# State space chunks: ScalarE scales both batches' states ahead of its copy of batch 0's transposes

## The chip, the cores and the metric

One core of a Trainium2 chip runs the whole program in one launch. The metric is the device time of one execution in microseconds (us). Three executions of the kernel before took 903.69, 904.62 and 905.2 us; the median is 904.62 us.

## The reference

The program is a stack of four blocks over x (2 batches, 1024 positions, 256 features) and a context of 2 x 77 x 256: a gated recurrence with attention and a feed-forward net, an attention block with a bottleneck of four features, an attention with 16 heads, and a last block whose first half is the state space layer (Mamba-2) that this change touches:

```
def step(h, inp):
    dec, u, bt, ct = inp
    h = h * dec[:, :, None, None] + u[..., None] * bt[:, None, None, :]
    y = jnp.einsum('bhpn,bn->bhp', h, ct)
    return (h, y)
...
y = ys.transpose(1, 0, 2, 3) + D_skip[None, None, :, None] * xh
u = _rms(y.reshape(b, L, D_INNER) * jax.nn.silu(z), gnorm_w)
return resid + u @ out_proj_w
```

There are 8 heads of 64 channels with a state of 64 x 128 each, so one batch's state is 128 x 512 numbers. dec is exp(dt * A), one factor for each head and position.

## The kernel before

Activations lie feature-major: features on the 128 partitions, positions along the free dimension. The positions are worked through in two halves (j = 0, 1) of T = 512, and the state space layer cuts each half into four chunks of 128 positions (s = 0 to 3). Within a chunk the recurrence is done with matrices: a masked 128 x 128 decay matrix for each head gives what the chunk's own positions contribute, and the state carried over from the chunk before gives the rest. Both batches (b = 0, 1) go through together, each with its own four PSUM banks and its own tiles.

The order of the work is written out by hand in a generator, mamba_order, which every engine's program walks through: for each s the pieces s1 (b = 0), s1 (b = 1), s2 (0), s2 (1), s3 (0), s3 (1). Each engine takes its share of each piece in that order and waits on semaphores for the others. What each engine does in a piece for one batch:

- s1, TensorE: four transposes of the convolved input (L1477), one transpose of B and the product of B and C (L1479, L1480), then four short bf16 matmuls that build the exponents of the decay matrix. It waits for this batch's L2481 of the chunk before (semaphore yr).
- s1, ScalarE: in the kernel before, first the decay: eight instructions of 128x64 (L1931) write SE = STATE times one factor for each head; they wait for the new state (L2476, semaphore s7). Then XT = the copy of the transposes out of PSUM (L1937), BT = the copy of B's transpose (L1939), and the exponential of the decay matrix, 128x1024 (L1941).
- s1, GpSimd: WX = XT times a factor (L822, 128x512); it waits for the copy L1937 and is waited for by TensorE's state update in s2. XT, WX and the factors WM all lie in SBUF.
- s2, VectorE: the decay matrix times the product of B and C (L2470), the carried part of y (L2472), and STATE = SE + the new contribution in PSUM (L2476; L2478 in the very first chunk). TensorE: four matmuls with the state (they wait for L1941 and for L2476 of the chunk before), then one with BT and WX.
- s3, TensorE: eight matmuls with the decay matrices (after L2470). VectorE: L2481 adds them to y out of PSUM, four scalar_tensor_tensor instructions of 128x128 (L2485) add D_skip times x, and L2487 multiplies by the gate. L2485 and L2487 each read two tensors from SBUF; L2470, L2472, L2476 and L2481 read one from SBUF and one from PSUM. A self-wait stands between L2472 and L2476, between L2481 and L2485, and between L2485 and L2487.

In the first chunk of the second half (j = 1, s = 0) both batches' decays already come together, after batch 1's exponential; they serve that same chunk. The first chunk of all (j = 0, s = 0) has no decay. So six chunks have the decay at the head of s1: s = 1, 2, 3 of either half.

After the four chunks of a half, piece "out" squares, normalises and projects the result.

Of the kernel before, what the change touches and what calls it, by code (L numbers as in the profile page):

```python
# [112 lines left out]
def xattn_stack_kernel(nc, xT, ctxT, mask, maskc, vecs, m0, m1, m2, rows6, consts, outT):  # L113
    vcol, nvec, mats, sizes = layout()
    with ExitStack() as ctx:
# [65 lines left out]
        def sem(name):  # L181
            name = home.get(name, name)
            if name not in sems:
                sems[name] = ctx.enter_context(nc.semaphore(name))
            return sems[name]

        def after(name, n):

            return sem(name), n + before.get(name, 0)
# [20 lines left out]
        def cn(name, rows=P):  # L210
            return CN[0:rows, CONST[name][0]:CONST[name][1]]
# [230 lines left out]
        def bank(b, k):  # L442
            return ps[:, 4 * b + k, :]
# [4 lines left out]
        def part_of(q):  # L448

            return q % B, slice(q // B * T, (q // B + 1) * T)  # L450
# [5 lines left out]
        BS = range(B)  # L456
# [278 lines left out]
        def inbank(b, j, k):  # L735

            return bank(b, (k + 2) % 4 if (j, b) == (0, 0) else k % 4)

        def of(name, b):

            return name + "01"[b]
# [821 lines left out]
        def _(act):  # L1563
# [194 lines left out]
            for q in UNITS[B:]:  # L1758
                b, span = part_of(q)
# [23 lines left out]
            for q in UNITS[:B]:  # L1783
                b, span = part_of(q)
                act.wait_ge(*after("rep_mm", q + 1))
                nc.scalar.activation(USR[:, b, span], ps[:, q, :], ACT.Copy).then_inc(sem("us"), 1)
            for q in UNITS[B:]:
                b, span = part_of(q)
# [60 lines left out]
            for piece, b, j, s in mamba_order():  # L1849
# [16 lines left out]
                elif piece == "xm":  # L1866
                    for u in BS:
                        act.wait_ge(*after("norm_xc", CENTRED["x3"] + B + u + 1))
                        nc.scalar.activation(ST[u], XC[u], ACT.Square).then_inc(sem("norm_sq"), 1)
                elif piece == "xq":  # L1870
                    for u in BS:
                        act.wait_ge(*after("norm_ms", NORMS["x3"] + B + u + 1))
                        nc.scalar.activation(RTB[u], bank(1, u), ACT.Ln, bias=cn("eps5")).then_inc(sem("norm_ln"), 1)
                        act.wait_ge(*after("norm_ln", NORMS["x3"] + B + u + 1))
                        nc.scalar.activation(RTB[u], RTB[u], ACT.Exp, scale=-0.5).then_inc(sem("norm_rt"), 1)
                elif piece == "sq":
                    act.wait_ge(*after("x3", 4 * J))
                    for u in BS:
                        nc.scalar.activation(SQ7[u], X[:, :, u, T:2 * T], ACT.Square).then_inc(sem("norm_sq"), 1)
                elif piece == "nb":  # L1880
                    for u in BS:
                        act.wait_ge(*after("norm_ms", NORMS["r3"] + u + 1))
                        nc.scalar.activation(RT7[u], ps[:, 6 + u, :], ACT.Ln, bias=cn("eps5")).then_inc(sem("norm_ln"), 1)
                        act.wait_ge(*after("norm_ln", NORMS["r3"] + u + 1))
                        nc.scalar.activation(RT7[u], RT7[u], ACT.Exp, scale=-0.5).then_inc(sem("norm_rt"), 1)
                elif piece == "dt":
                    act.wait_ge(sem("dt1"), 1)
                    nc.scalar.activation(ETR, ETR, ACT.Exp, scale=-1.0).then_inc(sem("et"), 1)
                    act.wait_ge(sem("et"), 1)
                    nc.scalar.activation(ETR, ETR, ACT.Ln, bias=cn("ones")[:, 0:1]).then_inc(sem("l1p"), 1)  # L1890
                elif piece == "rows":
                    prep_act(act, "a3")
                    act.wait_ge(sem("rows_mm"), 1)
                    nc.scalar.activation(RN[0], ps[:, 6, :], ACT.Copy).then_inc(sem("ltm"), 1)
                    act.wait_ge(sem("rows_mm"), 2)
                    nc.scalar.activation(WM.rearrange("p s n -> p (s n)"), ps[:, 5, :], ACT.Copy)
                    act.wait_ge(sem("een_mm"), 1)
                    nc.scalar.activation(EEN.rearrange("p s n -> p (s n)"), ps[:, 7, :], ACT.Exp).then_inc(sem("een"), 1)
                elif piece == "sel":
                    act.wait_ge(*after("sel_mm", j + 1))  # L1900
                    for i in range(4):
                        nc.scalar.activation(BX[j][:, i, :], ps[:, 3, :], ACT.Identity, bias=cn("unit")[:, i:i + 1], scale=cn("pick")[:, i:i + 1])
                    nc.scalar.activation(AE[j], ps[:, 3, :], ACT.Identity, bias=cn("first"), scale=cn("later")).then_inc(sem("ab"), 1)
                elif piece == "gate":
                    def convolved(b):
                        act.wait_ge(*after(of("cv", b), XBC * (j + 1)))
                        nc.scalar.activation(CV[b][:, 0:4, :], CV[b][:, 0:4, :], ACT.Silu)  # L1907
                        nc.scalar.activation(CV[b][:, 4:XBC, :], CV[b][:, 4:XBC, :], ACT.Silu).then_inc(sem(of("xs", b)), 1)

                    if j == 0 and b:  # L1910
                        convolved(0)
                    for c in range(4):
                        act.wait_ge(*after(of("in_mm", b), 10 * j + XBC + c + 1))
                        nc.scalar.activation(ZF[b][:, c, :], inbank(b, j, XBC + c), ACT.Silu).then_inc(sem(of("iev", b)), 1)
                        if b and c == (1 if j else 0):
                            convolved(1)
                    if j and b == 0:
                        convolved(0)
                    if b or j == 0:
                        nc.scalar.preload_act_table_set("natural_log_exp_and_others")  # L1920
                elif piece == "ef":
                    act.wait_ge(*after(of("ef_mm", b), j + 1))
                    for k in (2, 0):
                        nc.scalar.activation(EF[b][:, k:k + 2, :], ps[:, 4 * b + k:4 * b + k + 2, :], ACT.Exp).then_inc(sem(of("ef", b)), 1)  # L1924
                elif piece == "s1":
                    def decay(b):
                        act.wait_ge(*after(of("s7", b), n))
                        for h in range(HM):
                            head = slice(h * PD, (h + 1) * PD)
                            col = 32 * (B * j + b) + h  # L1930
                            ins = nc.scalar.activation(SE[b][:, head], STATE[b][:, head], ACT.Copy, scale=EEN[:, s, col:col + 1])  # L1931
                        ins.then_inc(sem(of("se", b)), 1)

                    if s:
                        decay(b)
                    act.wait_ge(*after(of("xt_mm", b), n + 1))
                    nc.scalar.activation(XT[b], bank(b, 0), ACT.Copy).then_inc(sem(of("dtx", b)), 1)  # L1937
                    act.wait_ge(*after(of("g7_mm", b), n + 1))
                    nc.scalar.activation(BT[b], bank(b, 1)[:, 0:P], ACT.Copy).then_inc(sem(of("bt", b)), 1)  # L1939
                    act.wait_ge(*after(of("dm_mm", b), n + 1))  # L1940
                    nc.scalar.activation(DM[b], ps[:, 4 * b + 2:4 * b + 4, :].rearrange("p k (h n) -> p (k h) n", h=4), ACT.Exp).then_inc(sem(of("dme", b)), 1)  # L1941
                    if s == 0 and j and b:
                        for u in BS:
                            decay(u)
                elif piece == "out":
                    act.wait_ge(*after(of("y7", b), SUB * j + SUB))
                    nc.scalar.activation(EF[b], ZF[b], ACT.Square).then_inc(sem(of("sq", b)), 1)
                    if j and b == 0:
                        act.wait_ge(sem("l3_ms"), B)
                        for u in BS:  # L1950
                            nc.scalar.activation(RTL[u], RTL[u], ACT.Ln, bias=cn("eps5")).then_inc(sem("l3_ln"), 1)
                        act.wait_ge(sem("l3_ln"), B)
                        for u in BS:
                            nc.scalar.activation(RTL[u], RTL[u], ACT.Exp, scale=-0.5).then_inc(sem("norm_rt"), 1)
                    act.wait_ge(*after(of("ms", b), j + 1))
                    nc.scalar.activation(RN[b], bank(b, 0), ACT.Ln, scale=1.0 / DI, bias=cn("eps5")).then_inc(sem(of("rl", b)), 1)
                    act.wait_ge(*after(of("rl", b), j + 1))
                    nc.scalar.activation(RN[b], RN[b], ACT.Exp, scale=-0.5).then_inc(sem(of("rr", b)), 1)
# [647 lines left out]
```

## Time and profile before

| what | value |
|---|---|
| median of three runs | 904.62 us |
| profiled execution, its own time | 905.31 us |
| its span | 903.2 us |
| mean granted TensorE clock | 0.994 of full speed |
| TensorE matmul busy | 840.6 us (93%) |
| VectorE busy | 517.3 us (57%) |
| ScalarE busy | 450.2 us (50%) |
| GpSimd busy | 48.5 us (5%) |
| L1931, the decay: 112 instructions | 28.0 us, mean 342 ns |
| L822, WX: 16 instructions | 1040 to 1380 ns, median 1042 ns |

Span is the time from the first to the last instruction; the execution's own time includes what lies around it. Busy shares are averages over the whole program, most of which is not the state space layer; the chunks take about 40 us in either half (from 655 to 696 us and from 757 to 801 us of the span). A row of the timeline gives the start, the duration, the engine and line, what is written from what, how many instructions were merged, and in brackets the idle time before it and what ended that. PEld is TensorE's loading of weights.

### The profile page before, as it was taken

What the parts mean: (1) busy time and instruction counts of PE and PEld (TensorE: products, weight loads), DVE (VectorE), ACT (ScalarE), POOL (GpSimd) and SP (SyncE); (2) the same over time, 40 slices, a digit from 0 to 9 for tenths busy, and PEclk for the clock granted to TensorE, in tenths of its full rate; (3) what the DMA queues carried; (4) which work ended last, traced back from release to release, by engine and by line L of the source; (5) the groups of instructions that cost most, each with busy time, mean ns of one, the idle gap of its engine ahead of it and who ended that gap; (6) DMA issues with size and microseconds to landing.
All of it is one profiled execution on the core that took longest, in us unless ns stands there. A gap on an engine that the chain in (4) does not pass through costs nothing.

```text
span 903.2 us, 10354 instructions
## 1 busy us (share of the span) xinstructions
PE 840.6 (93%) x4287; PEld 384.5 (43%) x4290; DVE 517.3 (57%) x714; ACT 450.2 (50%) x662; POOL 48.5 (5%) x41
## 2 busy tenths in 40 slices
PE   6998999999899999998898998999888999888987
PEld 2545444444344445453324244234455444544342
DVE  3378999843431031177636035479789495984442
ACT  3785222554434125353442723657875568652634
POOL 1000000020000000012200000000021000210000
PEclk9998999999999999999999999999999999999999
DMA  7000000011000000030000000000000000000011
GB/s 293 1 1 1 0 0 1 20 75 46 2 0 1 0 1 0 1 139 0 1 1 2 1 1 1 1 0 1 0 2 1 0 1 1 1 1 1 1 48 47
DMA packets 3005, 15.62 MB, mean 17 GB/s; under 512 B 656, under 2 KB 912, under 8 KB 2320
## 3 DMA queue, kind: packets, MB, share of 16 engines
q1 hardware_dynamic: 2816, 12.88, 3.8%
q0 software_dynamic: 144, 2.10, 0.6%
q8 instruction: 34, 0.56, 0.3%
q14 instruction: 11, 0.09, 0.0%
HBM read 12.87 MB, written 2.10 MB: 17 GB/s over the span
## 4 chain that ended last, share of the span: by engine, by line
PE 71%; ACT 15%; DVE 10%; DMA 2%; issue 1%; SPq 0%; POOL 0%; DVEq 0%; ACTq 0%
PE ps L421 70%; DVE VB L669 3%; ACT AR L653 3%; DMA WA<-in_m 2%; ACT AR L1941 2%; ACT AR L1931 1%; DVE AR L2254 1%; ACT AR L1625 1%; DVE AR L685 1%; ACT AR L1907 1%; ACT AR L658 1%; ACT AR L656 1%; DVE AR L511 1%; ACT AR L1924 1%; ACT AR L1937 1%
## 5 line engine op out<-in xcount | busy, mean ns | idle before, releaser
L421 PE MATMUL ps<-AR,WA 128*128 128x512 f32 (+2 forms) x716 | 307.8, 594 | 6.2 <-DVE AR L2487 3.6
L421 PEld LDWEIGHTS ps<-AR,WA 128*128 128x128 f32 (+2 forms) x716 | 130.4, 188 | 172.1 <-issue 157.6
L421 PE MATMUL ps<-AR,CN 128*128 128x512 f32 (+3 forms) x304 | 102.5, 598 | 2.8 <-DVE AR L1990 1.2
L421 PE MATMUL ps<-AR 128*64 128x128 f32 (+4 forms) x704 | 96.8, 402 | 6.2 <-ACT AR L1941 2.0
L685 DVE TENSOR_TENSOR AR<-ps,AR 128x512 f32<-128x512 f32 x24 | 16.6, 692 | 99.4 <-ACT AR L658 99.4
L421 PEld LDWEIGHTS ps<-AR 128*64 128x64 f32 (+3 forms) x704 | 51.1, 158 | 44.0 <-issue 19.4
L653 ACT ACTIVATE AR<-ps 77x2048 f32<-77x2048 f32 x24 | 44.0, 1870 | 42.2 <-PE ps L421 31.1
L669 DVE TENSOR_REDUCE VB<-ps 128x16 f32<-128x1232 f32 x32 | 44.9, 1438 | 29.4 <-PE ps L421 28.6
L421 PEld LDWEIGHTS ps<-AR,CN 128*128 128x128 f32 (+2 forms) x304 | 35.3, 157 | 50.9 <-issue 35.1
L2384 DVE SCALAR_TENSOR_TENSOR AR<-AR,VC 128x512 f32<-128x512 f32 x72 | 50.6, 749 | 5.4 <-ACT AR L1865 4.4
L1642 ACT ACTIVATE AR<-ps 128x512 f32<-128x512 f32 (+1 forms) x40 | 23.8, 597 | 59.1 <-DVE AR L2099 36.1
L421 PE MATMUL ps<-KB,WA 128*128 128x512 f32 (+1 forms) x120 | 51.4, 594 | 0.9 <-ACT AR L1924 0.9
L1739 ACT ACTIVATE AR<-ps,VC 128x512 f32<-128x512 f32 x32 | 21.9, 687 | 56.0 <-PE ps L421 56.0
L421 PE MATMUL ps<-CN 128*128 128x204 f32 (+6 forms) x102 | 41.0, 510 | 8.9 <-DMA CN<-in_consts 5.2
L2172 DVE SCALAR_TENSOR_TENSOR X<-ps,VC,X 128x512 f32<-128x512 f32 x8 | 5.6, 747 | 58.5 <-PE ps L421 58.5
L421 PE MATMUL ps<-AR,VS 77*32 77x512 f32 x256 | 32.4, 601 | 4.0 <-ACT AR L653 3.9
L421 PEld LDWEIGHTS ps<-KB,WA 128*128 128x128 f32 (+1 forms) x120 | 21.5, 184 | 29.4 <-issue 27.8
L421 PE MATMUL ps<-VB,CN 32*77 32x512 f32 x256 | 33.2, 587 | 0.0
L1931 ACT ACTIVATE AR<-AR,VB 128x64 f32<-128x64 f32 x112 | 28.0, 342 | 4.3 <-DVE AR L2476 2.9
L2099 DVE TENSOR_TENSOR_SCAN AR<-AR 128x512 f32<-128x512 f32 x24 | 29.5, 1272 | 0.4
L421 PEld LDWEIGHTS ps<-CN 128*128 128x128 f32 x102 | 17.9, 200 | 25.9 <-issue 13.0
L2470 DVE TENSOR_TENSOR AR<-AR,ps 128x1024 f32<-128x1024 f32 x16 | 19.4, 1216 | 15.9 <-ACT AR L1941 15.9
(334 smaller groups left out, 1126.0 us busy)
## 6 DMA issues: line engine op xcount, KB each, us to landing
WA<-in_m SPq DMA_DIRECT2D x1, 2856.0 KB, 9.7
WA<-in_m SPq DMA_DIRECT2D x1, 2560.0 KB, 15.6
X<-in_xT POOLq DMA_DIRECT2D x1, 2048.0 KB, 9.3
WA<-in_m SPq DMA_DIRECT2D x1, 2048.0 KB, 8.8
out<-X SPq DMA_DIRECT2D x4, 512.0 KB, 3.1
WB<-in_m SPq DMA_DIRECT2D x1, 1024.0 KB, 4.8
AR<-in_rows SPq DMA_DIRECT2D x1, 640.0 KB, 9.9
WA<-in_m SPq DMA_DIRECT2D x1, 512.0 KB, 16.4
```

The source lines that it names most:

```text
L421: return nc.tensor.matmul(out, lhsT, rhs, start=first, stop=last)
L511: nc.vector.tensor_tensor(xc[b], src(b), bc(at(b, 0), DC, 1), ALU.subtract).then_inc(sem("norm_xc"), 1)
L653: nc.scalar.activation(PTX[b][:, k], ps[0:M, 4 * b:4 * b + 4, :], ACT.Exp, bias=bias).then_inc(sem("att_ex"), 1)
L669: nc.vector.tensor_reduce(where[:, :, :, i] if PARTS[p] == 1 else where[:, :, 2 * k:2 * k + 2, 2 * g:2 * g + 2], ps[:, 4 * b:4 * b + 4, 0: ...
L685: nc.vector.tensor_tensor(ST[b][:, g, :], bank(b, 0), RTB[b], ALU.mult).then_inc(sem("att_ctx"), 1)
L1642: nc.scalar.activation(to[b][mo], bank(b, 2 * jj + mo), ACT.Sigmoid).then_inc(sem("g"), 1)
L1739: nc.scalar.activation(FH[b][item], bank(b, i % 2), ACT.Gelu_apprx_tanh, bias=v("bf1", item)).then_inc(sem("ff"), 1)
L1931: ins = nc.scalar.activation(SE[b][:, head], STATE[b][:, head], ACT.Copy, scale=EEN[:, s, col:col + 1])
L1941: nc.scalar.activation(DM[b], ps[:, 4 * b + 2:4 * b + 4, :].rearrange("p k (h n) -> p (k h) n", h=4), ACT.Exp).then_inc(sem(of("dme", b)), 1)
L2099: nc.vector.tensor_tensor_scan(dst[:, mo, b, jj, span], aa[b][:, mo, :], gz[b][:, mo, :], first, ALU.mult, ALU.add).then_inc(sem("h"), 1)
L2384: ins = STT(out=CV[b][:, k, :], in0=XB[b][:, k, tap:tap + T], scalar=v("convw", 4 * k + tap), in1=CV[b][:, k, :], op0=ALU.mult, op1=ALU.add)
L2470: TT(DM[b], DM[b], bc(bank(b, 1)[:, P:2 * P], HM, 1), ALU.mult).then_inc(sem(of("dm", b)), 1)
```

## The change

In the chunks s = 1, 2, 3 of either half, ScalarE issues both batches' decays ahead of batch 0's copy of the transposes, and none ahead of batch 1's. In s1 of batch 0 it therefore now also waits for batch 1's L2476 of the chunk before. Nothing else is changed; the first chunks of the halves stay as they are.

```
                     if s:
-                        decay(b)
...
+                    for u in BS if s and b == 0 else ():
+                        decay(u)
                     act.wait_ge(*after(of("xt_mm", b), n + 1))
                     nc.scalar.activation(XT[b], bank(b, 0), ACT.Copy).then_inc(sem(of("dtx", b)), 1)
```

(The line `if s:` is removed along with the call under it.) The function decay(b), unchanged:

```
def decay(b):
    act.wait_ge(*after(of("s7", b), n))
    for h in range(HM):
        head = slice(h * PD, (h + 1) * PD)
        col = 32 * (B * j + b) + h
        ins = nc.scalar.activation(SE[b][:, head], STATE[b][:, head], ACT.Copy, scale=EEN[:, s, col:col + 1])
    ins.then_inc(sem(of("se", b)), 1)
```

## Rows read from the trace of the kernel before

**Rows 1.** The chain that ended last, from 770 to 800 us, shares by line

```profile
by line: PE ps L421 40.6%; ACT AR L1941 19.4%; ACT AR L1931 19.0%; ACT AR L1937 4.8%; PE ps L1477 3.9%; DVE AR L2485 3.8%; DVE AR L2487 2.3%; DVE AR L2476 2.3%; DVE AR L2481 2.3%; ACT AR L1939 1.6%; DVE AR L2472 1.1%; issue 0.9%; PE ps L147
```

**Rows 2.** Timeline of one chunk: start, us, engine, line, count, [idle before <-releaser]

```profile
777.04 0.69 DVE L2476 TENSOR_TENSOR AR<-AR,ps 128x512 f32<-128x512 f32 x1
777.71 0.69 DVE L2481 TENSOR_TENSOR AR<-AR,ps 128x512 f32<-128x512 f32 x1
778.43 1.14 DVE L2485 SCALAR_TENSOR_TENSOR AR<-AR,VC 128x128 f32<-128x128 f32 x4
...
778.47 0.66 PE L1477 MATMUL ps<-CN,AR 128*128 128x128 f32 x4
...
779.16 0.60 ACT L1937 ACTIVATE AR<-ps 128x512 f32<-128x512 f32 x1 [1.83 <-PE ps L1477]
779.61 0.69 DVE L2487 TENSOR_TENSOR AR<-AR 128x512 f32<-128x512 f32 x1
...
779.83 1.36 POOL L822 TENSOR_TENSOR AR<-AR,VB 128x512 f32<-128x512 f32 x1 [5.22 <-ACT AR L1937]
780.22 0.68 DVE L2481 TENSOR_TENSOR AR<-AR,ps 128x512 f32<-128x512 f32 x1
780.25 1.02 ACT L1941 ACTIVATE AR<-ps 128x1024 f32<-128x1024 f32 x1 [0.32 <-PE ps L421]
780.93 1.20 DVE L2485 SCALAR_TENSOR_TENSOR AR<-AR,VC 128x128 f32<-128x128 f32 x4
...
780.95 0.66 PE L1477 MATMUL ps<-CN,AR 128*128 128x128 f32 x4 [0.75 <-DVE AR L2481]
781.17 2.01 ACT L1931 ACTIVATE AR<-AR,VB 128x64 f32<-128x64 f32 x8
```

**Rows 3.** The same chunk's timeline, its second half

```profile
782.17 0.69 DVE L2487 TENSOR_TENSOR AR<-AR 128x512 f32<-128x512 f32 x1
...
782.78 1.21 DVE L2470 TENSOR_TENSOR AR<-AR,ps 128x1024 f32<-128x1024 f32 x1
783.08 0.58 ACT L1937 ACTIVATE AR<-ps 128x512 f32<-128x512 f32 x1
...
783.74 1.04 POOL L822 TENSOR_TENSOR AR<-AR,VB 128x512 f32<-128x512 f32 x1 [2.54 <-ACT AR L1937]
783.91 0.69 DVE L2472 TENSOR_TENSOR AR<-ps,AR 128x512 f32<-128x512 f32 x1
784.73 0.69 DVE L2476 TENSOR_TENSOR AR<-AR,ps 128x512 f32<-128x512 f32 x1
784.78 1.19 PEld L421 LDWEIGHTS ps<-AR 128*128 128x128 f32 x10 [0.97 <-ACT AR L1941]
785.34 1.21 DVE L2470 TENSOR_TENSOR AR<-AR,ps 128x1024 f32<-128x1024 f32 x1
785.46 2.02 ACT L1931 ACTIVATE AR<-AR,VB 128x64 f32<-128x64 f32 x8 [0.73 <-DVE AR L2476]
786.47 0.68 DVE L2472 TENSOR_TENSOR AR<-ps,AR 128x512 f32<-128x512 f32 x1
...
787.19 0.69 DVE L2476 TENSOR_TENSOR AR<-AR,ps 128x512 f32<-128x512 f32 x1
```

**Rows 4.** Timeline elsewhere: a long GpSimd instruction and a VectorE instruction behind it

```profile
415.54 5.04 POOL L810 TENSOR_TENSOR X<-X,AR 128x2048 f32<-128x2048 f32 x1 [12.96 <-ACT AR L1778]
```

**Rows 5.** VectorE's timeline at that instruction's end

```profile
419.77 0.96 DVE L2249 TENSOR_SCALAR WA<-WA,VC 128x256 f32<-128x256 f32 x1
```

**Rows 6.** All of line L2249: duration ns min/median/max, first and last start

```profile
L2249 DVE TENSOR_SCALAR WA<-WA,VC x4: 341/342/962, 419.8 to 421.2; 128x256 f32<-128x256 f32 x4
```

**Rows 7.** Timeline of the second half's start, chunks s = 0 and 1

```profile
762.34 5.85 ACT L1931 ACTIVATE AR<-AR,VB 128x64 f32<-128x64 f32 x24
...
770.07 0.68 DVE L2481 TENSOR_TENSOR AR<-AR,ps 128x512 f32<-128x512 f32 x1
...
770.78 1.20 DVE L2485 SCALAR_TENSOR_TENSOR AR<-AR,VC 128x128 f32<-128x128 f32 x4
```

More of the change, by code:

```diff
@@ L1932, in decay @@
                         ins.then_inc(sem(of("se", b)), 1)
-                    if s:
-                        decay(b)
+                    for u in BS if s and b == 0 else ():
+                        decay(u)
                     act.wait_ge(*after(of("xt_mm", b), n + 1))
```

## The prediction

> **What bounds the kernel now.** I read three views. The chain of waits through the second half's chunks [rows 1] puts 19.0% on the decay (L1931) and 19.4% on the exponential behind it (L1941). That is the case for the change: TensorE's weight load for batch 1's state matmuls sits idle 0.97 us until L1941 of batch 1 is done, at 784.78 [rows 3], that exponential and its copy follow the decay of batch 1 (781.17 to 783.18) [rows 2, 3], and ScalarE itself idles 1.83 us ahead of batch 0's copy at 779.16 [rows 2]. Moving 2 us of decay into that hole looks like a gain of 0.97 us in each of six chunks, 5.8 us.
>
> The second view, VectorE's timeline over one chunk [rows 2, 3], says otherwise. Its twelve groups start 0.67, 0.72, 1.18, 0.61, 0.71, 1.24, 0.61, 1.13, 0.82, 0.61, 1.13 and 0.72 us after each other, from L2476 of batch 1 (777.04) round to the next (787.19): 10.15 us, with no hole. An unhindered step behind a 0.69 us instruction is 0.61 us (779.61 to 780.22) or, where a self-wait stands between, 0.72 us (786.47 to 787.19). So only two places wait for somebody: L2481 of batch 0 (0.67 for 0.61, on TensorE) and L2476 of batch 0 (0.82 for 0.72, on TensorE's state update). VectorE is the bound; the chain view followed a cycle that is within 0.2 us of VectorE's, and shows only the one that came last.
>
> The third view is GpSimd's two instructions in the same rows. WX of batch 1 (783.74) takes 1.04 us; WX of batch 0 (779.83) takes 1.36 us, beside L2487 of batch 0 (779.61 to 780.30). It ends at 781.19, which is 1.04 us after 780.15: it stood still until 0.15 us before L2487's record ended. L2487 lost nothing (0.69 us, as the other one at 782.17). Then the first of batch 1's four L2485 starts while WX still runs (780.93 against 781.19), and the four take 1.20 us where batch 0's take 1.14: 0.06 us lost.
>
> **The change step by step.** Take the same chunk and keep L2476 of batch 1 at 777.04.
>
> 1. Removed: the decay between batch 0's exponential and batch 1's copy. Batch 1's copy can start when its transposes are done, and the exponential when its exponents are: TensorE's weight load no longer waits 0.97 us. What is late next is VectorE, which isn't moved by that except at L2481 of batch 0: up to 0.06 us gained. The 0.10 us at L2476 of batch 0 stays, since its state update follows batch 1's transposes in TensorE's queue, and those follow L2481 of batch 1. Without anything else the chunk would take 10.09 us, and six chunks give 0.36, about 0.4 us.
>
> 2. Added: batch 1's decay ahead of batch 0's copy. It waits for L2476 of batch 1, which ends at 777.73, plus 0.04 us (784.73 + 0.69 to 785.46): start 777.77. Batch 0's decay is over by then (785.46 + 1.91 is before 787.19 + 0.69). From the decay's start to the copy's is 1.91 us (781.17 to 783.08), so batch 0's copy starts at 779.68 instead of 779.16, 0.52 us late. Queued behind it on ScalarE are B's copy and the exponential of batch 0, now ending about 781.4; TensorE wants that exponential only after batch 1's exponents, some 1.3 us after the 780.95 start of its transposes, so this is hidden. Who waits for the copy itself is GpSimd.
>
> 3. Moved with it: WX of batch 0. It starts 0.66 us after the copy (783.08 to 783.74): 780.34. L2487 of batch 0 now stands at 779.55 to 780.24, so WX is no longer held up, and ends at 781.38 instead of 781.19. Batch 1's L2485 starts at 780.87. What does it lose? Two rows bound it. Before, an overlap of 0.26 us cost 0.06, which as a share (0.23) makes 0.12 us of the new overlap of 0.51. At the other end is a GpSimd instruction at 415.54 that ends at 420.58 [rows 4], with a VectorE instruction behind it that starts at 419.77 and takes 0.96 us [rows 5] where the same line otherwise takes 0.34 [rows 6]: it stood still 0.62 us, until 420.39, which is 0.19 us before GpSimd's record ends. By that reading, L2485 stands still until 781.38 - 0.19 = 781.19, 0.32 us. It fits the small loss too: 781.19 - 0.19 is 781.00, and L2485 should have begun at 780.93, which is 0.07. I take 0.32.
>
> 4. Moved as well: WX of batch 1. Batch 1's L2481 stands at 780.16, its transposes start 0.73 later (780.22 to 780.95), the copy 0.69 after that (778.47 to 779.16), WX 0.67 after that: 782.25. L2487 of batch 1 comes at 780.87 + 0.32 + 1.17 = 782.36. GpSimd is ahead by 0.11 us. L2487, with both inputs in SBUF, then stands still until 782.25 + 1.04 - 0.19 = 783.10: 0.74 us. Before, this WX ran at 783.74 beside L2470 and L2472, which have one input in PSUM and lost nothing (1.21 and 0.69 us with it and without it). The bounds are nothing, if L2487 gets in first, and 0.85, if GpSimd is a whole release ahead; 0.74 is the one that the timing gives.
>
> So VectorE's round becomes 10.15 - 0.06 - 0.10 (both waits are swallowed) - 0.07 + 0.32 + 0.74 = 10.98 us, 0.83 more. Everything in it is counted from L2476 of batch 1, so it repeats; five of the six chunks have this pattern: 4.15 us.
>
> 5. The sixth, s = 1 of the second half. There ScalarE is behind: 24 decays in a row end at 768.19 [rows 7]. Eight more end past 770.0, batch 0's copy starts at 770.00 and WX at 770.66, while L2485 comes at 770.78: it stands still until 771.51, 0.73 us. Batch 1's WX then starts at about 772.23, amid the four L2485, and stops the next one until 773.08, some 0.77 us. That is 1.50 - 0.07 - 0.16 = 1.27 us.
>
> **Sum**: 4.15 + 1.27 = 5.4 us. Nothing hides it: TensorE's output projection waits for the last L2487, and TensorE is busy nearly without a break from there on. Against the profiled execution, 905.31 becomes 910.7; that execution lies 0.7 above the median, so the forecast is 904.62 + 5.4 = 910.0 us. TensorE's clock stands at 0.994 on average with waits of this length in the chunks already; I price it at nothing.
>
> The step that the rows leave open is the small overlap in 3: it can be read as a share or as a lock. The Trainium skill, SBUF — State Buffer, section "Who interferes with whom", says that a VectorE instruction with two SBUF inputs contends with a GpSimd instruction that reads SBUF, that the first to issue holds the shared ports for its whole length, and that the other blocks. By that rule the sum is the 5.4 us above; by a share it is rival B. The trace agrees with the rule in the 0.62 us stop [rows 5, 6], though there with a tensor_scalar.
>
> **Rivals.**
>
> A. L2487 of batch 1 gets in ahead of WX. The margin is 0.11 us, built from five steps read to 0.01 us each, and GpSimd's spans are rough. Then only 0.32 is lost: 10.24 us a chunk, 0.09 more, times five, plus the 1.27 of step 5: +1.7 us, 906.3. For it: the small margin. Against: L2485's own stop pushes L2487 back by the 0.32 that decides the race; below 0.21 it would turn.
>
> B. VectorE and GpSimd share rather than lock. Losing 0.23 of each overlap, L2485 gives 0.12 and L2487 0.16: 9.92 + 0.28 = 10.20, +0.05 a chunk, or at the other end nothing lost and the 0.36 of step 1 gained. Time 904.2 to 905.2. Against it: L2487 lost nothing while WX lost 0.32, and the 0.62 us stop.
>
> C. The chain view is right, and the 0.97 us comes off each chunk: 898.8 us. Against it: VectorE's round has 10.15 us with only 0.16 of waits and 0.07 of stop. Even with all of them gone it is 9.92, which caps the gain at 6 x 0.23 = 1.4 us, 903.2. It would need VectorE's steps to shrink.
>
> That the change doesn't do what it says would need batch 1's state to be late; it ends 1.4 us before the copy was due, so the decays do move.
>
> **How the numbers follow.** A measurement of this kernel can tell about 0.2%, 1.8 us, from no change. Forecast 0.64, A 0.13, B 0.19, C 0.04. Slower by over 0.2%: the forecast and a quarter of A, 0.67. Same: the rest of A and B, 0.29. Faster: C, 0.04. The range reaches from B's middle, 904.5, through A to 911.4, the forecast with 0.85 in place of 0.74 in five chunks (0.55) and the spread of the runs (0.75). The forecast's own range is 908.3 to 911.4.
>
> **What would show it.** Right: the first L2485 of batch 1 at about 0.67 us for 0.35 and L2487 of batch 1 at about 1.4 us for 0.69; both WX at 1.04 us; about 11.0 us from chunk to chunk; TensorE's wait on batch 1's L1941 gone, and a longer one on L2481. Wrong: L2487 of batch 1 at 0.69 us with a WX of over 1.3 us beside it (A), or a round of 10.1 us (B), or of 9.9 or less (C).

## The result and the profile after

The changed kernel takes 913.42 us in the median of seven executions (910.48 to 915.59), against 905.17 us for the kernel before on the same chips. The ratio is 1.0083, with a 95% interval from 1.0059 to 1.0107: 8.2 us slower, where 5.4 were forecast and the range ended at 911.4. The direction and the mechanism in the chunks hold; the size does not, since a term that was put at nothing is missing.

| what | before | after |
|---|---|---|
| profiled execution, its own time | 905.31 us | 915.59 us |
| its span | 903.2 us | 913.4 us |
| mean granted TensorE clock | 0.994 | 0.987 |
| VectorE busy | 517.3 us | 522.6 us |
| ScalarE busy | 450.2 us | 450.7 us |

The timeline of one chunk after, in the second half, from the L2476 of batch 1 that starts the count to the next one [answers to rows 2 and 3]:

```profile
782.43 0.69 DVE L2476 TENSOR_TENSOR AR<-AR,ps 128x512 f32<-128x512 f32 x1
783.04 0.68 DVE L2481 TENSOR_TENSOR AR<-AR,ps 128x512 f32<-128x512 f32 x1
783.15 2.02 ACT L1931 ACTIVATE AR<-AR,VB 128x64 f32<-128x64 f32 x8 [0.43 <-DVE AR L2476]
783.75 1.14 DVE L2485 SCALAR_TENSOR_TENSOR AR<-AR,VC 128x128 f32<-128x128 f32 x4
...
784.93 0.69 DVE L2487 TENSOR_TENSOR AR<-AR 128x512 f32<-128x512 f32 x1
785.08 0.57 ACT L1937 ACTIVATE AR<-ps 128x512 f32<-128x512 f32 x1
...
785.54 0.68 DVE L2481 TENSOR_TENSOR AR<-AR,ps 128x512 f32<-128x512 f32 x1
...
785.73 1.04 POOL L822 TENSOR_TENSOR AR<-AR,VB 128x512 f32<-128x512 f32 x1 [8.39 <-ACT AR L1937]
786.25 1.46 DVE L2485 SCALAR_TENSOR_TENSOR AR<-AR,VC 128x128 f32<-128x128 f32 x4
...
787.64 1.04 POOL L822 TENSOR_TENSOR AR<-AR,VB 128x512 f32<-128x512 f32 x1 [0.87 <-ACT AR L1937]
787.74 1.49 DVE L2487 TENSOR_TENSOR AR<-AR 128x512 f32<-128x512 f32 x1
...
791.00 0.69 DVE L2476 TENSOR_TENSOR AR<-AR,ps 128x512 f32<-128x512 f32 x1
...
793.45 0.69 DVE L2476 TENSOR_TENSOR AR<-AR,ps 128x512 f32<-128x512 f32 x1
```

Read it against [rows 2, 3]. WX of batch 0 (785.73) now takes 1.04 us instead of 1.36 and ends at 786.77. Batch 1's four L2485 take 1.46 us instead of 1.20: 0.32 more than batch 0's undisturbed 1.14. WX of batch 1 starts at 787.64, L2487 of batch 1 0.10 us behind it at 787.74, and that takes 1.49 us for 0.69. From one L2476 of batch 1 to the next are 11.02 us, 10.15 before. GpSimd gained, VectorE lost: both WX have their shortest time, and every VectorE instruction with two SBUF inputs that begins beside one waits until it is nearly done. By the 0.19 us of the working L2487 would end at 789.18 (787.64 + 1.04 - 0.19 + 0.69); its record ends at 789.23, so it went on only 0.14 us before WX's record ends.

The chunk s = 1 of the second half, where ScalarE is behind [rows 7]:

```profile
766.41 7.76 ACT L1931 ACTIVATE AR<-AR,VB 128x64 f32<-128x64 f32 x32
...
774.72 1.04 POOL L822 TENSOR_TENSOR AR<-AR,VB 128x512 f32<-128x512 f32 x1 [8.11 <-ACT AR L1937]
774.86 2.63 DVE L2485 SCALAR_TENSOR_TENSOR AR<-AR,VC 128x128 f32<-128x128 f32 x4
...
776.27 1.06 POOL L822 TENSOR_TENSOR AR<-AR,VB 128x512 f32<-128x512 f32 x1 [0.51 <-ACT AR L1937]
```

The four L2485 take 2.63 us, 1.49 more than undisturbed (1.50 in the working), stopped once by each WX.

So far everything is as forecast. One chunk of this trace is not: in s = 1 of the first half GpSimd lost the race.

```profile
668.14 0.69 DVE L2487 TENSOR_TENSOR AR<-AR 128x512 f32<-128x512 f32 x1
...
668.29 1.44 POOL L822 TENSOR_TENSOR AR<-AR,VB 128x512 f32<-128x512 f32 x1 [1.12 <-ACT AR L1937]
```

WX of batch 1 came 0.15 us behind L2487, and it is WX that was stopped (1.44 us); the four L2485 took 1.21 us, and the chunk 10.09 us instead of 11.02. TensorE's clock was low just ahead of it (0.50 from 655 to 660 us), VectorE waited for TensorE, and so came to its instructions at other moments against GpSimd's. So in this execution the chunks cost 4.7 us more than before, not 5.4.

The rest is outside the chunks. TensorE's timeline behind the last chunk of each half, first before, then after:

```profile
695.85 3.70 PE L421 MATMUL ps<-AR,WA 128*128 128x512 f32 x8 [1.82 <-DVE AR L2487]
...
800.67 3.70 PE L421 MATMUL ps<-AR,WA 128*128 128x512 f32 x8 [1.81 <-DVE AR L2487]
```

```profile
698.44 5.40 PE L421 MATMUL ps<-AR,WA 128*128 128x512 f32 x8 [2.73 <-DVE AR L2487]
...
807.72 5.40 PE L421 MATMUL ps<-AR,WA 128*128 128x512 f32 x8 [2.73 <-DVE AR L2487]
```

The same eight matmuls of the output projection take 5.40 us instead of 3.70, in both halves. TensorE waited 2.73 us ahead of them instead of 1.8: its work in the last chunk is done earlier, since it no longer waits for batch 1's exponential, while VectorE's L2487 of batch 0 comes when VectorE gets there. Busy time by stretch, with the granted clock in the column behind the engines, for the changed kernel:

```profile
695.00:700.00 5.00, 2.27 (x17) 1.30 (x14) 4.86 (x13) 1.58 (x1) 0.00 (x0) 0.94 0.00 0
700.00:705.00 5.00, 5.00 (x10) 2.00 (x9) 1.99 (x3) 0.33 (x1) 0.00 (x0) 0.72 0.00 0
805.00:810.00 5.00, 2.28 (x4) 1.16 (x5) 4.86 (x13) 2.31 (x2) 0.00 (x0) 0.86 0.00 0
810.00:815.00 5.00, 5.00 (x10) 2.01 (x9) 3.66 (x4) 2.11 (x5) 1.80 (x1) 0.80 0.02 3
```

In the kernel before the stretches around these matmuls stand at 1.00. Here the clock went from 2.4 to 1.2 GHz behind TensorE's wait (cut into single microseconds: 1.00 up to 699, 0.50 from 700 to 702) and came back during the projection (1.00 from 703). This trace also has such a stretch from 655 to 660 us (0.50), ahead of anything that the change moves; the kernel before has some of its own, in other places (0.73 to 0.92 between 70 and 85 us). They come and go from execution to execution, and single times of one kernel scatter over 6 us and more with them (an execution of the kernel before at a clock of 0.997 took 902.3 us, one at 0.984 took 911.5). The profiled executions differ by 10.3 us, the medians by 8.2.

### The profile page after: what moved, and what is told of

The parts are those of the page before. It is cut to its first block, busy times and chain, and to the rows that moved or that the text cites. A ratio compares the mean times of both kernels' runs of the same rounds, so it can differ in the third digit from the quotient of the medians.

```text
span 913.4 us, 10357 instructions
## 1 busy us (share of the span) xinstructions
PE 846.1 (93%) x4290; PEld 387.5 (42%) x4290; DVE 522.6 (57%) x714; ACT 450.7 (49%) x662; POOL 47.1 (5%) x41
## 4 chain that ended last, share of the span: by engine, by line
PE 71%; DVE 15%; ACT 11%; issue 2%; DMA 1%; SPq 0%; POOL 0%; DVEq 0%; ACTq 0%
PE ps L421 69%; DVE VB L669 3%; ACT AR L653 3%; DMA CX<-in_ctxT 1%; DVE AR L2485 1%; DVE AR L2254 1%; DVE AR L2481 1%; DVE AR L2470 1%; ACT AR L1625 1%; DVE AR L2476 1%; DVE VB L2099 1%; DVE AR L685 1%; DVE AR L2487 1%; ACT AR L1907 1%; ACT AR L658 1%
## 5 line engine op out<-in xcount | busy, mean ns | idle before, releaser
L421 PE MATMUL ps<-AR,WA 128*128 128x512 f32 (+2 forms) x716 | 311.2, 599 | 6.9 <-DVE AR L2487 5.5
L421 PE MATMUL ps<-AR,CN 128*128 128x512 f32 (+3 forms) x304 | 104.4, 604 | 2.9 <-DVE AR L1990 1.2
L421 PE MATMUL ps<-AR 128*64 128x128 f32 (+4 forms) x704 | 99.1, 407 | 6.4 <-ACT AR L1941 2.0
L421 PEld LDWEIGHTS ps<-AR 128*64 128x64 f32 (+3 forms) x704 | 53.6, 162 | 44.0 <-issue 21.9
L2470 DVE TENSOR_TENSOR AR<-AR,ps 128x1024 f32<-128x1024 f32 x16 | 19.4, 1214 | 15.9 <-ACT AR L1941 15.9
```

The costliest lines, as they stand in the source:

```text
L421: return nc.tensor.matmul(out, lhsT, rhs, start=first, stop=last)
L2470: TT(DM[b], DM[b], bc(bank(b, 1)[:, P:2 * P], HM, 1), ALU.mult).then_inc(sem(of("dm", b)), 1)
```

## The experiments

Each run was timed beside the kernel before on the same chip; ratios have 95% intervals. "A chunk" is the time from one L2481 of batch 0 to the next, in steady state: 10.16 us before, 11.02 in the changed kernel. Unless something else is said the edit is made to the changed kernel.

### Does GpSimd's WX stop VectorE?

**e1_gate_wx1** makes WX of batch 1 wait for L2487:

```
+                    if b and 4 * j + s:
+                        pool.wait_ge(*after(of("y7", 1), 4 * j + s))
                     nc.gpsimd.tensor_tensor(h3(WX[b]), ...
```

> The changed kernel, with one wait more: GpSimd's WX of batch 1 waits for VectorE's L2487 of batch 1 of the chunk before. Lock theory (an instruction of GpSimd and one of VectorE with two SBUF inputs exclude each other, first come first served): L2487 of batch 1 back from 1.49 to 0.69 us, the four L2485 of batch 1 still at 1.46, chunk to chunk 10.24 us instead of 11.02, no stop of 0.8 in the chunk s = 1 of the second half. In the chunks 4.4 us less than the changed kernel. If the cost of the clock behind the chunks hangs on TensorE's wait of 2.7 us there, which this edit leaves as it is, it stays: about 4 us above the kernel before; if that was chance, about 1 us above. Rival (the order of ScalarE's work itself costs the time, by way of TensorE): nothing gained over the changed kernel, 8 us above before.

Measured: 907.24 us, ratio 1.0025 (1.0009 to 1.004), about 1.8 us above before. A chunk takes 10.22 us; the chunk s = 1 of the second half takes 10.6. In its timeline, where the lines stand two further down (L2487 is the four additions, L2489 the gate product):

```profile
770.41 1.04 POOL L824 TENSOR_TENSOR AR<-AR,VB 128x512 f32<-128x512 f32 x1 [8.11 <-ACT AR L1939]
770.55 1.83 DVE L2487 SCALAR_TENSOR_TENSOR AR<-AR,VC 128x128 f32<-128x128 f32 x4
...
772.42 0.69 DVE L2489 TENSOR_TENSOR AR<-AR 128x512 f32<-128x512 f32 x1
...
773.25 1.04 POOL L824 TENSOR_TENSOR AR<-AR,VB 128x512 f32<-128x512 f32 x1 [1.80 <-DVE AR L2489]
```

The gate product is back at 0.69 us in all sixteen places; the stop of the four additions by WX of batch 0 stays (1.83 here, 1.46 in the other chunks but the first half's s = 1, which again stands behind a stretch at the lower clock, with 1.20). One added wait gives back 0.80 of the 0.86 us a chunk. ScalarE's order is unchanged in this run, so the order by itself isn't what costs the time. The wait behind the chunks came out at 2.28 and 2.29 us, not at the 2.7 that the text assumed, and the eight matmuls behind both took 3.70 us; the total lies between the text's two cases.

**e2_gate_both** makes both WX wait (the same two lines without `b and`).

> The changed kernel, with both WX waiting for L2487 of batch 1 of the chunk before. Lock theory: no VectorE instruction is held up any more: L2485 of batch 1 at 1.14 and L2487 at 0.69 us; but WX of batch 0 is now late for TensorE's state update, L2476 of batch 0 waits some 0.4 us, and a chunk takes about 10.4 us. 1.7 us above the kernel before, plus 3 if the clock falls behind the chunks. Rival: as the changed kernel.

Measured: 909.65 us, ratio 1.0047 (1.0023 to 1.0071). No VectorE instruction is held up: 1.14 and 0.69 us everywhere. But a chunk takes 10.60 us, since L2476 of batch 0 now waits for WX by way of TensorE:

```profile
785.15 2.04 POOL L824 TENSOR_TENSOR AR<-AR,VB 128x512 f32<-128x512 f32 x2 [8.56 <-DVE AR L2489]
786.05 0.68 DVE L2474 TENSOR_TENSOR AR<-ps,AR 128x512 f32<-128x512 f32 x1
786.25 4.78 PE L421 MATMUL ps<-AR 128*128 128x512 f32 x44 [0.26 <-POOL AR L824]
787.47 0.69 DVE L2478 TENSOR_TENSOR AR<-AR,ps 128x512 f32<-128x512 f32 x1 [0.73 <-DVE AR L2474]
```

The 0.73 us ahead of 787.47 is that wait (the view names the instruction in front of it). The forecast of 10.4 was 0.2 low. Behind the chunks TensorE waited 2.14 us twice, and once the eight matmuls took 5.40 us.

**e3_wx_memset** takes the reading away from GpSimd:

```
-                    nc.gpsimd.tensor_tensor(h3(WX[b]), h3(XT[b]), bc(WM[...], PD, 2), ALU.mult)...
+                    nc.gpsimd.memset(WX[b], 0.0)...
```

> The changed kernel with WX written by a memset of the same shape instead of the product (leaves out the product of XT and its factors, so the state stays zero): GpSimd reads nothing from SBUF. Lock theory: L2485 of batch 1 at 1.14 and L2487 at 0.69 us wherever the memset runs, a chunk takes 10.09 us, 0.4 us below the kernel before over the six chunks; plus 3 us if the clock falls behind the chunks, since TensorE's wait there stays near 2.7 us. Rival (a delay from ScalarE's order): a chunk still takes 11.0 us.

Measured: 905.33 us, ratio 1.0009 (0.9984 to 1.0034). A chunk takes 10.08 us (10.09 expected):

```profile
766.99 0.53 POOL L822 MEMSET AR<- 128x512 f32 x1 [8.63 <-ACT AR L1937]
767.14 1.14 DVE L2485 SCALAR_TENSOR_TENSOR AR<-AR,VC 128x128 f32<-128x128 f32 x4
...
776.68 0.52 POOL L822 MEMSET AR<- 128x512 f32 x1 [7.62 <-ACT AR L1937]
...
777.22 1.14 DVE L2485 SCALAR_TENSOR_TENSOR AR<-AR,VC 128x128 f32<-128x128 f32 x4
...
778.39 0.69 DVE L2487 TENSOR_TENSOR AR<-AR 128x512 f32<-128x512 f32 x1
...
778.59 0.53 POOL L822 MEMSET AR<- 128x512 f32 x1 [1.39 <-ACT AR L1937]
```

The pair at 766.99, in the chunk s = 1 of the second half, is the test: the memset was there first, the additions began 0.15 us behind it, and they take 1.14 us, where a stop until 0.20 us before the memset's end would have cost 0.18. In the chunk at 776.68 the first memset ends just ahead of the additions, so there the shorter instruction does as much as the missing read. The second begins 0.20 us behind L2487, which would have won against a WX as well; it shows that a memset isn't stopped in its turn (0.53 us). With GpSimd out of the way the new order is worth 0.08 us a chunk: that is all that TensorE's 0.97 us of waiting had ever cost.

**e7_split** cuts batch 1's decay in two, so that neither WX moves into VectorE's way (the edit is shown against the kernel before; the helper takes the heads as a second argument):

```
+                    if s and b == 0:
+                        decay(0)
+                        decay(1, range(4))
+                    elif s:
+                        decay(1, range(4, HM))
```

> The changed kernel with batch 1's decay cut in two: four heads ahead of batch 0's copy, four ahead of batch 1's. Batch 0's copy is then no later than in the kernel before, and batch 1's copy comes 0.5 us later than in the changed kernel, so that its WX would start about 0.05 us behind L2487 of batch 1. Lock theory: L2487 of batch 1 at 0.69 us, WX of both batches at 1.36 us, the four L2485 of batch 1 at 1.20, a chunk takes 10.09 us: 0.4 us below the kernel before. If WX of batch 1 gets in first after all, L2487 shows 1.4 us and a chunk 10.9. Rival (ScalarE's order costs the time): a chunk between 10.2 and 11.0 with no long VectorE instruction.

Measured: 907.21 us, ratio 1.0026 (0.9997 to 1.0056). Inside the chunks it is as expected to 0.02 us: 10.07 to 10.08 us a chunk, the additions of batch 1 at 1.21, the gate product at 0.69. Here WX of batch 0 came behind the gate product of batch 0 and waited for it:

```profile
789.34 0.69 DVE L2491 TENSOR_TENSOR AR<-AR 128x512 f32<-128x512 f32 x1
...
789.56 1.38 POOL L822 TENSOR_TENSOR AR<-AR,VB 128x512 f32<-128x512 f32 x1 [6.08 <-ACT AR L1941]
```

WX of batch 1 started only as the gate product of batch 1 ended, and took 1.04 us, where 1.36 was expected. The total isn't what the chunks give: it lies 2.2 us above the kernel before, where 0.4 below was expected. The mean granted clock of its twelve runs was 0.990, and the 0.5 us that the chunks gained can't be seen beside that.

### Where do the other 2 us come from?

**a1_after_again** is the changed kernel once more; **a2_after_look** and **a3_after_look** are one traced execution of it each.

> The changed kernel once more, for a second trace and for its clock beside that of the kernel before on one chip. Lock theory: 11.02 us from chunk to chunk, 11.4 into the chunk s = 1 of the second half, L2487 of batch 1 at 1.49 us in five chunks or, if the half's start is delayed by the clock, in four. Clock theory: a mean granted clock some 0.002 to 0.003 below the kernel before, and of the two waits of 2.7 us behind the chunks at least one followed by eight matmuls that take 5.4 us instead of 3.7; about 8 us above the kernel before. Rival (the clock's share of the first measurement was chance): the same clock as before, and 5.5 us above.

> The changed kernel, one look for the clock behind the chunks. Clock theory: of the two waits of 2.7 us for L2487 at least one is followed by a fall of the granted clock, eight matmuls in 5.4 us instead of 3.7.

> As a2_after_look: a fall behind at least one of the two waits of 2.7 us. If three or more of the four waits of these two looks show none, the clock falls there by chance, and the cause of its share stays open.

Measured: 912.52 us, ratio 1.008 (1.0054 to 1.0106); the two single executions took 913.53 and 912.38 us. The trace of a1_after_again has no stretch at the lower clock ahead of or in its chunks, and so shows their price cleanly: 11.01, 11.01, 11.02 us in the first half and 11.39, 11.01, 11.02 in the second, for 10.13, 10.16, 10.16 and 10.14, 10.16, 10.16 before. That is 5.55 us more; the forecast had 5.42. Behind its chunks:

```profile
695.14 3.70 PE L421 MATMUL ps<-AR,WA 128*128 128x512 f32 x8 [2.72 <-DVE AR L2487]
...
802.91 5.40 PE L421 MATMUL ps<-AR,WA 128*128 128x512 f32 x8 [2.73 <-DVE AR L2487]
```

Over the four traces of the changed kernel there are seven waits of 2.72 to 2.73 us, and five are followed by matmuls at the lower clock (an eighth was 2.11 us long, since TensorE's clock had fallen in the chunk ahead of it). Two waits a run, five times in seven, 1.7 us each, is 2.4 us. Over all its 19 runs the mean granted clock is 0.9903, that of 95 runs of the kernel before, beside the experiments, 0.9932; the medians are 912.66 and 905.05. The difference of 7.6 us less 5.5 leaves 2.1, or 2.5 if the first half's s = 1 escapes the stops in half of the executions, as in two of the four traces (10.09 and 10.08 us). a3_after_look shows one more place where the clock falls: in the last chunk of its second half the four transposes of batch 1 took 1.12 us instead of 0.66, L2487 came ahead of WX (0.69 us, with a WX of 1.24 us beside it), and the chunk took 13.25 us instead of 11.02, as VectorE waited for TensorE. In e4_spare_again, below, the same chunk took 11.66 us. Two of the seven traces with chunks of 11.0 us have such a fall behind a half's first chunk; neither of the two traces with the order of the kernel before has (before, e6_before_spare). That the fall comes for certain, which the first text expected of at least one wait a run, is refuted by a3_after_look: none there behind its one wait of 2.7 us.

**e4_spare**, **e4_spare_again** and **e8_one_spare** give TensorE something to do in that wait, matmuls of 512 columns whose result nobody reads (e8 has one `spare(3, T)` instead of the loop of two):

```
                     last.then_inc(sem(of("y1_mm", b)), 1)
+                    if s == SUB - 1 and b:
+                        pe.wait_ge(*after(of("s7", 0), n + 1))
+                        for u in range(2):
+                            spare(3, T)
```

> The changed kernel with two spare matmuls of 512 columns on TensorE at the end of each half's last chunk, into a bank nobody reads. Clock theory (the granted clock falls behind the chunks since TensorE waits 2.73 us for L2487, 1.8 before): TensorE's wait there is about 1.0 us, the first eight matmuls of the output projection take 3.7 us (5.4 in the changed kernel), the clock of those stretches is 1.00, and the kernel is some 3 us faster than the changed one: 5.4 us above the kernel before. The chunks stay at 11.02 us. Rival (the clock falls at random): no steady gain over the changed kernel.

> The changed kernel with two spare matmuls at the end of each half's last chunk, measured again for its clock. If TensorE's wait of 2.7 us there is what lowers the clock (19 runs of the changed kernel have a mean of 0.9903, 82 of the kernel before 0.9932): a mean clock of 0.992 to 0.993 and 6 us above the kernel before. If the longer waits inside the chunks lower it: 0.990 to 0.991 and 8 us above.

> The same with one spare matmul instead of two, so that TensorE's wait is 1.7 to 1.8 us, as in the kernel before. If that wait decides: the eight matmuls behind it take 3.7 us, a mean clock of 0.992 to 0.993, and 6 us above the kernel before. If not: as the changed kernel, 8 us above.

Measured: 910.59 us, ratio 1.006 (1.0038 to 1.0081); 910.91 us, ratio 1.006 (1.0038 to 1.0081); 910.57 us, ratio 1.0057 (1.0038 to 1.0077). With two spares the wait is 0.81 us (once 0.23, behind a chunk under a lower clock), and the projection's eight matmuls take 3.70 us in all four places traced. Those of e4_spare:

```profile
698.35 3.70 PE L421 MATMUL ps<-AR,WA 128*128 128x512 f32 x8 [0.81 <-DVE AR L2491]
...
806.13 3.70 PE L421 MATMUL ps<-AR,WA 128*128 128x512 f32 x8 [0.81 <-DVE AR L2491]
```

The chunks stay at 11.0 us. The 21 runs of the three have a mean clock of 0.9929 and a median of 910.6 us, 2.1 below the changed kernel's; drawing both sets of runs anew many times puts 95% of the differences between 1.1 and 3.5 us. The 15 runs with two spares alone give 1.9 us, between 0.3 and 3.7. What is left, 5.5 us above before, is what the chunks alone cost. The intervals of the single ratios still overlap, so the 2 us rest on the pooled runs and on the traces together. The one-spare kernel does not give the clean limit that its text looked for: its wait is 1.67 us, shorter than that of the kernel before, and one of two was followed by a fall all the same:

```profile
696.52 3.70 PE L421 MATMUL ps<-AR,WA 128*128 128x512 f32 x8 [1.67 <-DVE AR L2490]
...
804.35 5.40 PE L421 MATMUL ps<-AR,WA 128*128 128x512 f32 x8 [1.67 <-DVE AR L2490]
```

**e6_before_spare** adds the two spares to the kernel before.

> The kernel before with the two spare matmuls at the end of each half's last chunk, and nothing else. Clock theory with a limit between 1.8 and 2.7 us of waiting: the kernel before waits 1.8 us there and its clock holds, so the spares change nothing: within 0.1% of the kernel before. Rival (any wait there costs some of the runs their clock): up to 1 us faster in the median, and a mean clock above that of the kernel before.

Measured: 905.05 us, ratio 1.0007 (0.9984 to 1.0031): worth nothing that can be seen there, as the first text has it. The interval is 2 us wide to either side.

### A version that beats both

VectorE bounds the chunks, and ScalarE has 2 us a chunk to spare. **f1_scale_on_act** moves the multiplication by D_skip to it, so that VectorE adds once instead of four times, and holds both WX back:

```
+                    for u in BS if b else ():
+                        for c in range(4):
+                            xc = CV[u][:, c, s * P:(s + 1) * P]
+                            ins = nc.scalar.activation(xc, xc, ACT.Copy, scale=v("dskip", c))
...
-                    for c in range(4):
-                        yc = YT[b][:, c * P:(c + 1) * P]
-                        ins = STT(out=yc, in0=CV[b][:, c, sub], scalar=v("dskip", c), in1=yc, op0=ALU.mult, op1=ALU.add)
-                    ch.link(ins)
...
+                    ch.link(TT(c3d(YT[b]), CV[b][:, 0:4, sub], c3d(YT[b]), ALU.add))
```

> An attempt at a faster kernel, built on the changed one: ScalarE, which idles 2 us a chunk there, multiplies x by D_skip in place behind the exponentials (eight instructions of 128x128 a chunk), VectorE adds it in one instruction of 128x512 (0.69 us) instead of four L2485 (1.14), and both WX wait for the gate product of batch 1 of the chunk before, so that none meets a VectorE instruction with two SBUF inputs. If VectorE bounds the chunks: its round falls from 9.92 to 9.0 us, and the round through TensorE's state update becomes the bound at 9.64: a chunk takes 9.6 to 9.7 us, eight chunks 3 to 4 us, 901 to 902 us in all. Rival (ScalarE or TensorE bounds them, as the chain view says): 10 us a chunk or more.

Measured: 904.87 us, ratio 0.9995 (0.9968 to 1.0021). A chunk takes 9.70 us, as VectorE's bound says, but the chunk s = 1 of the second half takes 10.80 (with a granted clock of 0.71 from 765 to 770 us in it) and the mean clock was 0.990. The total is 3 us above what was expected.

**f2_reordered** and **f3_reordered_spare** let VectorE do L2481 of both batches first, so that TensorE gets on earlier:

```
+                    for u in BS if b else ():
...
+                        ins = TT(c3d(YT[u]), CV[u][:, 0:4, sub], c3d(YT[u]), ALU.add)
+                    if b:
+                        ch.link(ins)
+                    for u in BS if b else ():
+                        TT(ZF[u][:, :, sub], c3d(YT[u]), ZF[u][:, :, sub], ALU.mult)...
```

> The faster attempt once more, with VectorE releasing TensorE earlier: L2481 of both batches first, then the two sums with D_skip times x, then the two gate products; and in the first chunk of the second half the decays come ahead of ScalarE's new multiplications. If the round through TensorE's state update bounds f1 at 9.70 us, batch 1's transposes start about 0.6 us earlier against the rest and a chunk takes 9.3 us; six chunks 2.4 us and the second half's start 1 us less than f1: at the same granted clock 5 to 6 us below the kernel before, 899 to 900 us. Rival (ScalarE's 9 us of work bound it by now): 9.6 to 9.7 us a chunk, as f1.

> The same as f2_reordered with the two spare matmuls at the end of each half's last chunk. Clock theory: where TensorE's wait behind the chunks is 2 us or less the spares are worth nothing, within 0.1% of f2_reordered; if they raise the mean granted clock by 0.001, about 0.7 us less.

Measured: 905.79 us, ratio 1.0015 (0.9993 to 1.0036), and 904.69 us, ratio 0.9993 (0.9967 to 1.0018). A chunk takes 9.33 us, as expected, and the totals don't follow: the chunk s = 1 of the second half takes 13.44 us in f2 and 12.97 in f3, where the kernel before has 10.14. f3's spares cut TensorE's wait behind the chunks from 2.77 to 0.85 us; the 1.1 us between the two medians is inside the noise. The timeline at the second half's start of f2 shows where the gain went:

```profile
762.83 3.93 ACT L1933 ACTIVATE AR<-AR,VB 128x64 f32<-128x64 f32 x16
...
766.65 2.45 ACT L1950 ACTIVATE AR<-AR,VC 128x128 f32<-128x128 f32 x8
...
768.98 3.93 ACT L1933 ACTIVATE AR<-AR,VB 128x64 f32<-128x64 f32 x16
...
774.50 1.22 DVE L2477 TENSOR_TENSOR AR<-AR,ps 128x1024 f32<-128x1024 f32 x1 [2.63 <-ACT AR L1943]
774.52 7.14 PE L421 MATMUL ps<-AR 128*128 128x128 f32 x52 [2.31 <-ACT AR L1943]
```

ScalarE has two rounds of decays and the new multiplications one behind the other, 10 us of work; VectorE waits 2.63 us and TensorE 2.31 for the exponential behind them, and TensorE's 52 matmuls then take 7.14 us for 5.75, at a granted clock of 0.92 and 0.74 in the two stretches from 770 to 780 us.

**f4_best** takes that out: the first round of decays goes to VectorE, which is idle there.

```
+                    if s == 0 and j and b == 0:
+                        for u in BS:
...
+                            cols = 32 * (B * j + u)
+                            TT(h3(SE[u]), h3(STATE[u]), bc(EEN[:, s, cols:cols + HM], PD, 2), ALU.mult)...
```

> The faster attempt: as f2_reordered, but the last chunk of a half keeps the order by batch, so that the output projection starts no later; in the first chunk of the second half VectorE, idle there for 7 us, makes both batches' decays (two instructions of 128x512 instead of sixteen on ScalarE), which takes away the 1.6 us that L2476 waits there for ScalarE; and one spare matmul stands behind the chunks. The chunks of s = 2 and 3 at 9.3 us, s = 1 at 9.6. At the same granted clock 5 to 6 us below the kernel before, about 899.5 us; with a lower clock, as in f1 and f2 (0.990), some 2 us less gain. Rival (ScalarE's backlog in the second half's first chunks stays): 2 us below.

Measured: 896.44 us, ratio 0.9907 (0.9886 to 0.9928): 8.8 us faster than the kernel before, and 17 below the changed one's 913.42, with the reference's computation complete. In its timeline at the same place:

```profile
750.33 1.28 DVE L2481 TENSOR_TENSOR AR<-AR,VB 128x512 f32<-128x512 f32 x2
...
759.94 0.69 DVE L2491 TENSOR_TENSOR AR<-AR,ps 128x512 f32<-128x512 f32 x1 [0.23 <-PE ps L421]
...
763.00 1.28 DVE L2496 TENSOR_TENSOR AR<-AR,ps 128x512 f32<-128x512 f32 x2
...
772.33 1.28 DVE L2496 TENSOR_TENSOR AR<-AR,ps 128x512 f32<-128x512 f32 x2
```

Both decays take 1.28 us in time that VectorE had free, the wait of L2476 for them is 0.23 us instead of 1.64, and the chunks follow each other after 9.33 us. It gained more than forecast (899.5). Against the trace of before, the stretch from the first L2481 to the projection is 2.9 us shorter in the first half, and the one from the second half's first L2470 to the projection 4.3 us: 7.2 of the 7.6 us by which the two profiled executions differ. The mean clock of its five runs was 0.994, and none of the stretches in or behind its chunks is at the lower clock.

## Why the prediction was wrong

- **What bounds the chunks**: right. VectorE's round was the bound, and TensorE's wait of 0.97 us was worth 0.08 us a chunk when nothing else got in the way (e3, e7); the forecast had 0.06. That wait is gone, and TensorE waits 0.83 us for L2481 of batch 0 in its stead (at 783.78), as the signs had it.
- **Step 2**, batch 0's copy 0.52 us later: right. It starts 2.65 us behind L2476 of batch 1 (782.43 to 785.08); the working gives 2.64.
- **Steps 3 and 4**, the stops of L2485 and L2487: right, 0.32 and 0.80 us for 0.32 and 0.74. The race that decides step 4 was won by GpSimd with 0.10 us, forecast 0.11; the missing 0.05 us of the stop is that VectorE went on 0.14 us before WX's end and not 0.19. A chunk takes 11.02 us for 10.98. But "five of the six chunks have this pattern" holds only while TensorE's clock does: in after and a2_after_look the first half's s = 1 took 10.09 and 10.08 us, in a3_after_look the last chunk went the other way too.
- **Step 5**: right, 1.25 us in the clean trace for 1.27.
- **The sum of the chunks**: 5.55 us for 5.4. The lock reading against the share reading is settled for L2487 as well: losing 0.80 us beside a WX of 1.04 cannot be a share of 0.23. Rival A is refuted by the same row, B by that row and e1, C by the chunk time. Its picture, L2487 first and WX stopped, is what the odd chunks named above show, so the small margin was real.
- **The step that failed** is the sentence behind the sum: "TensorE's clock stands at 0.994 on average with waits of this length in the chunks already; I price it at nothing." The wait that grew to a new length was not one of those in the chunks. I counted what the new order takes from TensorE's wait inside a chunk and didn't follow it to the end of the half, where the same 0.9 us comes back as a longer wait ahead of the projection: 2.73 us for 1.8. The term belongs in the sum at about 2 us: 1.7 us each time, in five of seven traced waits. With it the forecast would have been 912, and a range as wide would have reached 913.4.
- **Two slips without weight**: the projection waits for batch 0's L2487 and not for "the last" (695.10 + 0.69 in the kernel before, and the matmuls start at 695.85); and the middle of rival B's 904.2 to 905.2 is 904.7, not 904.5.

The clock is only partly explained. That filling the wait gives back about 2 us is what the pooled runs and traces say together; that it is this wait and not also the falls inside a chunk, which the spares don't touch, is not settled. Nor is why e7, f1 and f2, whose waits behind the chunks are 2.1, 1.7 and 2.8 us, also had a mean clock of 0.990 (in f2's trace the clock fell behind one of its two waits and in a chunk, in f1's in a chunk, in e7's in neither); twelve runs each leave an uncertainty of about 0.001 in that mean.

## What to carry to other kernels

An engine that is "idle 2 us ahead of it" is not where the time is, if another engine goes round without a hole; lay out one full period of the busiest engine and count its gaps before moving work on the others. When a producer's time shifts, follow its consumers to GpSimd: an instruction there that reads SBUF, started 0.1 us ahead of a VectorE instruction with two SBUF inputs, stops it for nearly its own length (0.80 us of a WX of 1.04 here), and a wait on the VectorE instruction cures that at no cost where the result isn't needed yet (e1; in e2, where it was needed, it cost 0.4 us a chunk). And a wait taken from TensorE inside a loop comes back at the loop's end, where it can cost the clock as well.

## What was not expected of the hardware

The stop is the same to 0.01 us in every chunk that is at the full clock, and the record of the stopped instruction grows by it, so that it looks like a slow instruction and not like a wait. How early the stopped one goes on differs a little: VectorE's L2487 0.14 us before GpSimd's record ends, its L2485 0.20 us, the L2249 of [rows 5] 0.19; GpSimd's WX 0.13 to 0.15 us before VectorE's does. The Trainium skill, SBUF — State Buffer, section "Who interferes with whom", has the rule that the first to issue holds the shared ports and the other blocks; the trace agrees in both directions (1.49 us for 0.69 on VectorE, 1.38 for 1.04 on GpSimd in e7). A memset on GpSimd, which reads nothing, neither stops the additions nor is stopped by the gate product (e3). A series of short VectorE instructions is no protection: in the chunk s = 1 of the second half the second WX came in between two of the four L2485, which together took 2.63 us for 1.14.

The fall of TensorE's clock behind a wait is not a matter of that wait's length alone, though the long ones have it more often. Over all traces, the projection's eight matmuls took 5.40 us behind six of nine waits of 2.72 to 2.77 us (the changed kernel and f2), one of eight of 2.13 to 2.29 us (e1, e2, e3, e7), one of six of 1.67 to 1.82 us (before, e8, f1) and none of eight of 0.85 us or less (e4 twice, f3, f4).
